# The order of the four matmuls of a chunk in the down projection

## The reference, cut to what matters

```
def _qlinear(x, q, scale, A, Bm):
    w = (q.astype(jnp.float32) - Q_ZERO) * (scale * Q_STEP)[:, None]
    y = jnp.einsum('bsh,oh->bso', x, w)
    return y + LR_SCALE * (x @ A @ Bm)

g = _qlinear(x, gate_q, gate_scale, gate_A, gate_B)      # 512 -> 1376
u = _qlinear(x, up_q, up_scale, up_A, up_B)              # 512 -> 1376
h = jax.nn.silu(g) * u
return _qlinear(h, down_q, down_scale, down_A, down_B)   # 1376 -> 512
...
x = x + _L0_ffn_ref(_L0_cond_ref(x, ...), ...)
x = x + _L1_ffn_ref(_L1_cond_ref(x, ...), L1_ffn_weight)
```

## Time and profile before

| | us |
|---|---|
| median of 3 runs | 374.08 |
| the runs | 373.35 to 374.56 |
| the profiled execution's own time | 375.06 |
| its span, first to last instruction | 373.3 |
| TensorE busy with matmuls | 362.0 (97%) |
| TensorE busy with weight loads | 300.5 (81%) |
| VectorE busy | 245.5 (66%) |
| ScalarE busy | 190.6 (51%) |

### The profile page before, as it was taken

The page is one execution under the profiler, slowest core; times in us unless marked ns, Lnnn a source line. Parts: engine busy times, 40 slices in busy tenths (PEclk is TensorE's granted clock), DMA queues, the critical chain, the costliest instruction groups (busy, mean ns, idle before and its releaser), DMA issues.

```text
span 373.3 us, 5795 instructions
## 1 busy us (share of the span) xinstructions
PE 362.0 (97%) x2208; PEld 300.5 (81%) x2208; DVE 245.5 (66%) x410; ACT 190.6 (51%) x345; POOL 78.4 (21%) x67
## 2 busy tenths in 40 slices
PE   7998999999999999999999999999999999998994
PEld 3767887999888879998888889988888899997331
DVE  4958989726576665174766652637889922688994
ACT  4676798303565563035555541335667510067971
POOL 2100000011232233111332241113233221142030
PEclk9999999999999999999999999999999999999998
DMA  6889575396220000222200001426000299968188
GB/s 228 303 188 362 154 270 186 102 316 118 42 43 0 0 2 1 44 42 42 43 1 0 2 0 21 64 43 154 0 4 0 60 295 261 207 165 212 41 192 261
DMA packets 82475, 41.72 MB, mean 112 GB/s; under 512 B 52416, under 2 KB 72784, under 8 KB 82320
## 3 DMA queue, kind: packets, MB, share of 16 engines
q1 hardware_dynamic: 69072, 37.70, 37.2%
q10 hardware_dynamic: 12624, 1.82, 3.1%
q0 software_dynamic: 752, 1.84, 2.6%
HBM read 26.55 MB, written 14.80 MB: 111 GB/s over the span
## 4 chain that ended last, share of the span: by engine, by line
PE 89%; DVE 4%; DMA 3%; ACT 2%; issue 1%; POOL 0%; DVEq 0%; SPq 0%
PE ps L673 42%; PE ps L658 25%; PE ps L688 6%; PE ps L708 3%; PE ps L868 3%; PE ps L606 3%; DMA lr_b<-lr_b_rows 3%; PE ps L710 2%; PE ps L664 1%; PE ps L848 1%; PE ps L621 1%; DMA lr_b_rows<-lr_b_parts 1%; PE ps L566 1%; DVE v_plus L1505 1%; DVE q_fp L1524 1%
## 5 line engine op out<-in xcount | busy, mean ns | idle before, releaser
L658 PE MATMUL ps<-down_w,h_hi 128*128 128x288 f32 (+1 forms) x352 | 76.2, 297 | 0.0
L658 PE MATMUL ps<-down_w,h_lo 128*128 128x288 f32 (+1 forms) x352 | 74.7, 293 | 0.0
L673 PE MATMUL ps<-x_hi,gate_w 128*128 128x512 f32 (+1 forms) x176 | 69.9, 397 | 0.0
L673 PE MATMUL ps<-x_hi,up_w 128*128 128x512 f32 (+1 forms) x176 | 69.6, 395 | 0.0
L673 PE MATMUL ps<-x_lo,gate_w 128*128 128x512 f32 (+1 forms) x176 | 69.6, 395 | 0.0
L673 PE MATMUL ps<-x_lo,up_w 128*128 128x512 f32 (+1 forms) x176 | 69.3, 394 | 0.0
L1138 POOL TENSOR_TENSOR h_lo<-a_buf,h_hi 128x512 fp32r<-128x512 f32 (+1 forms) x33 | 42.9, 1299 | 90.0 <-ACT h_hi L979 90.0
L658 PEld LDWEIGHTS ps<-down_w,h_hi 128*128 128x128 f32 (+1 forms) x352 | 57.3, 189 | 1.0
L658 PEld LDWEIGHTS ps<-down_w,h_lo 128*128 128x128 f32 (+1 forms) x352 | 56.1, 188 | 0.0
L1434 DVE TENSOR_TENSOR a_buf<-a_buf,b_buf 128x512 f32<-128x512 f32 (+1 forms) x44 | 49.5, 1124 | 8.8 <-ACT a_buf L1043 7.7
L1149 POOL TENSOR_TENSOR x_nat<-y_buf,x_nat 128x512 f32<-128x512 f32 x15 | 20.8, 1385 | 116.4 <-DVE y_buf L1311 116.4
(11 more groups left out here) (195 smaller groups left out, 488.4 us busy)
## 6 DMA issues: line engine op xcount, KB each, us to landing
x_nat<-in_x SPq DMA_DIRECT2D x4, 1024.0 KB, 6.3
out<-x_nat SPq DMA_DIRECT2D x15, 256.0 KB, 4.2
turned<-x_nat SPq DMA_DIRECT2D x12, 256.0 KB, 3.3
x_nat<-in_down_q SPq DMA_DIRECT2D x11, 256.0 KB, 3.6
x_nat<-in_gate_q SPq DMA_DIRECT2D x10, 256.0 KB, 5.5
x_nat<-in_up_q SPq DMA_DIRECT2D x10, 256.0 KB, 5.7
edges<-zeros SPq DMA_DIRECT2D x4, 512.0 KB, 9.8
xt_own<-turned SPq DMA_DIRECT2D x6, 256.0 KB, 3.4
```

What stands on the lines that cost most here:

```text
L658: last = mm(ps[:, 4 + 2 * (j % 2) + m, 0:HALF + R], part[0:k, ic, j * P:(j + 1) * P], down_w[0:k, ic, m, :], start=first, stop=end)
L673: last = mm(ps[0:k, bank(ic, 2 * m), :], w[:, H * ic + c * k:H * ic + (c + 1) * k], part[:, c, :], start=c == 0 and part is x1_hi, stop=c ...
```

## The change

The two inner loops of a chunk trade places. Before, the four matmuls are `h_hi` with m = 0, `h_hi` with m = 1, `h_lo` with m = 0, `h_lo` with m = 1. After, they are `h_hi` with m = 0, `h_lo` with m = 0, `h_hi` with m = 1, `h_lo` with m = 1. Each bank still receives the same products in the same order, and the last matmul of a group, which carries `down_mm`, is the same one.

```
-                    for part in (h_hi, h_lo):
-                        first, end = ic == 0 and part is h_hi, ic == IC - 1 and part is h_lo
-                        for m in range(2):
+                    for m in range(2):
+                        for part in (h_hi, h_lo):
+                            first, end = ic == 0 and part is h_hi, ic == IC - 1 and part is h_lo
                             last = mm(ps[:, 4 + 2 * (j % 2) + m, 0:HALF + R], part[0:k, ic, j * P:(j + 1) * P],
                                       down_w[0:k, ic, m, :], start=first, stop=end)
                 last.then_inc(down_mm, 1)
```

## The result

| | before | after |
|---|---|---|
| median of 6 runs, us | 373.89 | 376.41 |
| the runs, us | 373.35 to 374.56 | 375.80 to 377.79 |
| the profiled execution's own time, us | 375.06 | 376.48 |
| its span, us | 373.3 | 374.7 |

The changed kernel is slower: the ratio is 1.0065, with a 95% interval of 1.0047 to 1.0083. The forecast was 374.1 us, no change. The time lies inside the range, 372.6 to 376.8, near its upper end.

What follows compares the result with a forecast made beforehand. The prediction took TensorE as the bound, with line 658's 704 matmuls back to back. Loads, differing weights, banks and waits each added 0 to the 374.08 us median, giving 374.1 us, range 372.6 to 376.8.

Steps and rivals of the forecast that it cites:

- rival B: Line 658's chunks: with unlike weights long loads come more often; +2.7 us at two a chunk, 376.8 us; chance 0.14.
- What bounds the kernel: Line 658 on TensorE: 704 matmuls run without idle, 133 ns apart, so each ns between starts counts 704 times.
- Number of loads: Line 658: 704 weight loads before, the same 704 after, 0 us.
- Weights that differ: Line 658: no load repeats the last one any more; taken as 0 us, with ends of -1.3 and +2.7 us.
- Banks: Line 658: two matmuls in a row adding into one bank cause no stall, 0 us; far end 56 us.
- rival C: Line 658: adding twice in a row into one bank stalls; +3.5 us at 10 ns a pair, 377.6 us; chance 0.06.
- Waits and marks: Around line 658: waits, the down_mm mark, VectorE's 21.4 us of waiting, transfers and other queues stay unchanged, 0 us.
- The sum of 0: All parts of the change together: 0 us against the median of 374.08 us, so 374.1 us.
- Rival A: Line 658: the long load belongs to the repeated load and goes; gain 1.3 us at most, 372.8 us; chance 0.17.
- slow and fast chunks: Line 658's two rhythms before: 533 ns a chunk ahead of the turn, 520 ns behind it; 100 slow, 76 fast.
- 100 long loads: Line 658: one load some 10 ns longer in each of 100 slow chunks; 373.2 us if only those 10 ns go.

Runs made afterwards that it cites:

- e5: Kernel before with weights h_hi, h_lo, h_hi, h_lo on moving halves 0, 1, 0, 1, banks 0, 1, 0, 1: ratio to before 0.9993, 60 matmuls in 7.97 us.
- e6: Kernel before with weights still in pairs, but moving halves and banks 0, 0, 1, 1: ratio to before 1.0044, 60 matmuls in 8.06 us.
- e1: Kernel before, old order of weights and moving halves, only the banks paired 0, 0, 1, 1: ratio to before 1.0008, 60 matmuls in 7.97 us.
- e2: Changed kernel, new order of weights and moving halves, only the banks alternating 0, 1, 0, 1: ratio to before 1.0048, 60 matmuls in 8.06 us.
- e7: Changed kernel with all four matmuls of a chunk loading h_hi, moving halves 0, 0, 1, 1: 376.25 us (one time), 60 matmuls in 8.06 us.
- f1: Changed kernel with the h_lo matmuls reading the half of the chunk before, 2,304 bytes earlier: 376.24 us (one time), 60 matmuls in 8.06 us.
- f2: Kernel before with down_w rows widened to 320 columns, 288 read, so all halves start alike modulo 256 bytes: ratio to before 1.0020, 60 matmuls in 8.00 us.
- f4: Changed kernel with down_w rows widened to 320 columns, a repeated run: ratio to before 1.0049, 60 matmuls in 8.00 us.

## Why the prediction was right, and where it was not

The time fell inside the range by luck: the range's upper end is the dear end of rival B, whose cause, unlike weights, the runs refute. The forecast of no change did not come, and slower by more than 0.3%, which came, had been given 0.18.

**What bounds the kernel: right.** Line 658 runs without a gap, and each ns between its starts counts. The mean distance rose by 0.48 us / 176 = 2.7 ns, over the 1.6 ns that the prediction named as the point where it fails as a forecast of no change.

**Number of loads: right.** 704 before and after.

**Weights that differ: right at 0;** e5 and e6 show it at 288 columns, where the rows of 512 columns could only suggest it. The ends put around it, -1.3 and +2.7 us, made the range wide enough, though the cost came from another side.

**Banks: right at 0.** e1 and e2 show it: e1 has the distances of before to 1 ns, so nothing is left for rival C.

**Waits and marks: right.** VectorE waited for line 658 for 21.4 us in 16 groups; now it is

```profile
DVE s_sum L1294 <- PE ps L658: 21.8, 16, 3.0
```

**The sum of 0: wrong, by 2.0 us in the trace and 2.5 us in the medians.** The step that failed is one that isn't there. The part on the change weighed the stationary side and the output, and never the moving side. Four matmuls have three operands each, and the change reorders the sequence of all three. What the runs showed in its place: the sequence of the moving operand's starting places alone took line 658 from 93.6 to 95.6 us. Rows 8 and 9 could not have caught it: the moving tiles there, `x1_hi` and `x1_lo`, have rows of 512 columns, 2,048 bytes, so that all of them start at one place modulo 256 bytes, and the equality of 232.5 ns says nothing of a sequence of two places.

**Rival B was the case that came, at 0.14,** in its outline only. Its place (each chunk of line 658), its sign and its observation (the rhythm depends on what stands where in the queue) were right. Its cause, unlike weights, was wrong, and so was its title: long loads came less often, 104 instead of 123. Its dear end, 2.7 us, was above the 2.0 us found in the trace and near the 2.5 us between the medians. It expected chunks of 543 ns throughout; they are some 520 to 560, 540 ahead of the turn and 546 behind it.

**Rival A** read the long loads as a property of repeated ones. Rows 6 and 11 allowed that, since a repeated load and the place beside the first matmul of a part are the same thing in the old order. Only an order that separates them (e5) tells. Its sign, loads of 187 to 188 ns alone, did not come either: the new order has no repeated load, and the stretch of the timeline above (148.6 to 150.9 us) still has loads of 191 and 193 ns.

```profile
L658 PEld LDWEIGHTS ps<-down_w,h_hi x9: 187/188/193, 148.5 to 150.8; 128*128 128x128 f32 x9
L658 PEld LDWEIGHTS ps<-down_w,h_lo x8: 187/188/191, 148.7 to 150.6; 128*128 128x128 f32 x8
```

**Two readings were off,** neither with weight in the sum. The 16 matmuls behind the turn are no mean of slow and fast chunks: the chunk right behind the turn is longer than either, 0.57 us from its start below to 151.06, and three fast ones follow. That they too come to 133 ns each is chance.

```profile
150.49 0.47 PE L658 MATMUL ps<-down_w,h_hi 128*128 128x288 f32 x2
```

And without the 10 ns of 100 long loads rival A stands at 374.1 - 1.0 = 373.1 us, not 373.2.

The chances leaned too much on no change. The two rhythms of one and the same sequence, 13 ns a chunk apart, were evidence that TensorE's distance reacts to something that the rows didn't name. A cause unseen there can be moved by a reordering, in either direction.

## What to carry to other kernels

When matmuls run back to back, a reordering changes three sequences: weights, output banks and moving addresses; cost each by itself, and test it by swapping one while holding the other two. Where a chunk reads two halves of a row, look at where each half starts: here alternating starts, 128 bytes apart modulo 256, ran at 132.8 ns a matmul in the first 60 of a tile, the same starts in pairs at 134.3, and padding to one place at 133.3. A regular small unevenness in a busy engine's rhythm is worth an experiment before a forecast of no change.

## What the runs showed of the hardware that was not expected

- The place where the moving columns start, modulo 256 bytes and relative to the matmul before, changes the distance between matmuls of 288 columns of 4 bytes: 60 of them take 7.97, 8.00, 8.04 or 8.06 us by the sequence alone, 132.8 to 134.3 ns each. The Trainium skill (TensorE: Matmul & The Clock Gate, Back-to-back issue gap) has, for an isolated matmul, a distance that depends on the number of columns alone; an estimate by its formula is 122.5 ns for 288 columns at the higher clock. The stream here is slower than that, and it depends on where the columns start as well.
- Which weights are loaded, `h_hi` or `h_lo`, has no influence here, not even if all four loads of a chunk bring in the same values (e7, 8.06 and 2.22 us as e6). Nor has the order of the two banks (e1 7.97 us as before, e2 8.06 as after), nor reading the same columns twice in a row (f1, 8.06 as after). The Trainium skill (TensorE: Matmul & The Clock Gate, Step-by-step: what each phase is for) gives TensorE two independent read ports, so that loading weights takes no read bandwidth from the matmul that runs. e6 and e7 agree as far as the choice of the weights goes; no run here shows the ports.
- These lengths repeat to 0.01 us in the first three tiles (in the fourth the bias stands within the 60), and between kernels with one sequence of places on different chips: 8.06 us in e6 and in f1, 8.00 us in f2 and in f4. The times of whole executions scatter by 0.5 us and more. A change of 0.5% is read far more surely from such a length than from a median.
